# Starting attention's first head inside the last two iterations of a Mamba and expert stage

## The reference, cut to what matters

```
x = _layernorm(x + _L0_attn_ref(x, ...), axis=-1)     # Mamba
x = _layernorm(x + _L0_ffn_ref(x, ...), axis=-1)      # router, 4 experts, top 2
x = _layernorm(x + _L1_attn_ref(x, ...), axis=-1)     # softmax(scores) @ v, 16 heads
x = _layernorm(x + _L1_ffn_ref(x, ...), axis=-1)
```

## Time and profile before

| what | us |
|---|---|
| median of 3 runs (lowest, highest) | 3949.27 (3946.3, 3962.15) |
| the profiled execution | 3957.01 |
| its span, first to last instruction | 3955.2 |
| TensorE busy (share) | 3451.3 (87%) |
| VectorE busy (share) | 2949.9 (75%) |
| ScalarE busy (share) | 2202.5 (56%) |
| GpSimd busy (share) | 1519.5 (38%) |
| mean granted TensorE clock, as a share of full speed | 0.934 |

### The profile page before, as it was taken

How to read it: one execution, slowest core, us unless ns; L and a number is a source line. 1 busy time by engine, 2 the same in 40 slices (tenths; PEclk the granted TensorE clock), 3 DMA queues, 4 the chain that set the end, 5 groups by cost and what they waited for, 6 DMA issues and landing times. The chain is left out here.

```text
span 3955.2 us, 50070 instructions
## 1 busy us (share of the span) xinstructions
PE 3451.3 (87%) x14561; PEld 1589.3 (40%) x14561; DVE 2949.9 (75%) x3567; ACT 2202.5 (56%) x3624; POOL 1519.5 (38%) x1292
## 2 busy tenths in 40 slices
PE   3348888898888889898958999999999999999898
PEld 1115545454554545455621233333223323233566
DVE  3898787888878787884128888888878888888343
ACT  4436555555556545554112777777777777777221
POOL 1988778787777878786010000000000000000110
PEclk8669999898999989999976999999999999999999
DMA  2111213121121312212103000000000000001000
GB/s 97 31 38 48 62 55 106 56 86 67 59 67 56 106 54 76 75 58 103 51 32 96 21 18 18 18 18 18 18 18 18 20 23 19 18 18 34 21 28 30
DMA packets 110953, 183.09 MB, mean 46 GB/s; under 512 B 14624, under 2 KB 84792, under 8 KB 102010
## 3 DMA queue, kind: packets, MB, share of 16 engines
q1 hardware_dynamic: 110713, 180.20, 14.3%
HBM read 154.05 MB, written 26.09 MB: 46 GB/s over the span
## 5 line engine op out<-in xcount | busy, mean ns | idle before, releaser
L1700 DVE TENSOR_REDUCE tile_max<-ps 128x1 f32<-128x1024 f32 x1076 | 1267.7, 1220 | 254.7 <-PE ps L1483 251.9
L1641 ACT ACTIVATE probs<-ps 128x512 f32<-128x512 f32 x2056 | 1116.2, 599 | 457.0 <-PE ps L1497 431.3
L1182 POOL TENSOR_TENSOR h<-h,c_sb 128x512 f32<-128x512 f32 x512 | 684.8, 1369 | 329.8 <-DVE state L996 329.7
L990 DVE TENSOR_TENSOR_SCAN h<-decay,state,ps 128x512 f32<-128x512 f32 x512 | 655.1, 1279 | 105.9 <-POOL y_sum L1193 34.1
L1497 PE MATMUL ps<-qs,ks 101*128 101x512 bf16 x2056 | 708.4, 382 | 1.2
L1483 PE MATMUL ps<-ks,qs 99*128 99x512 bf16 x2152 | 664.0, 390 | 49.0 <-DMA ks<-scratch_kb 41.1
L1193 POOL TENSOR_TENSOR y_sum<-y_sum,h 128x512 f32<-128x512 f32 x512 | 638.6, 1279 | 8.7 <-issue 0.2
L1817 POOL COPY vh<-v_all 128x256 f32 (+1 forms) x32 | 12.6, 400 | 1403.4 <-PE ps L1507 1339.8
L1507 PE MATMUL ps<-probs,vh 128*32 128x512 f32 x4096 | 545.6, 605 | 3.5 <-issue 3.5
L539 PE MATMUL ps<-x1T,e_w 128*128 128x512 f32 x1024 | 486.4, 626 | 58.5 <-ACT hid L807 58.5
L561 PE MATMUL ps<-e_w,hid 128*128 128x256 f32 x2048 | 455.4, 381 | 38.4 <-issue 19.0
(11 more groups left out here) (176 smaller groups left out, 2870.7 us busy)
## 6 DMA issues: line engine op xcount, KB each, us to landing
e_w<-in_e_w SPq DMA_DIRECT2D x64, 1024.0 KB, 7.0
c_sb<-scratch_c SPq DMA_DIRECT2D x128, 256.0 KB, 3.3
qs<-scratch_q SPq DMA_DIRECT2D x210, 64.0 KB
ks<-scratch_k SPq DMA_DIRECT2D x210, 64.0 KB
scratch_q<-parts SPq DMA_DIRECT2D x16, 384.0 KB, 4.0
scratch_k<-parts SPq DMA_DIRECT2D x16, 384.0 KB, 4.1
xr<-scratch_x SPq DMA_DIRECT2D x10, 512.0 KB, 4.2
xn_tok<-in_x SPq DMA_DIRECT2D x8, 512.0 KB, 4.9
```

The lines of the kernel that those rows point to most:

```text
L990: v.tensor_tensor_scan(h[:, n % 2, m, :], decay[:, n % 2, m, :], ps[:, 0, :], state[:, n, m:m + 1], ALU.mult, ALU.add).then_inc(s["h_ready ...
L1182: last = nc.gpsimd.tensor_tensor(h[:, n % 2, m, :], h[:, n % 2, m, :], c_sb[:, n % C_RING, :], ALU.mult)
L1641: fn(probs[:, step % 2, qc, :], ps[:, S_BANK[i], :], ACT.Exp)\
L1700: v.tensor_reduce(tile_max[:, t, half:half + 1], ps[:, slot(side):slot(side) + PAIR, :].rearrange("p a n -> p (a n)"), AX.X, ALU.max).then ...
```

## The change

A class `Shared` holds buffers and semaphores for both stages. `decay`, `delta` and `du` of the first stage lie in the memory of the stacks, `h`, `xb` and `pre` in that of the values, `y_sum` in that of the staged values. In iterations 8 and 9, where their first use is over, the second stage's run-up is done: VectorE fills the stacks' last rows (slot 3 of iteration 8), SyncE loads three stacks and the values of sequence 0 (slot 5), GpSimd stages the values of four heads (slot 8), and the 49 items are done by TensorE and VectorE in the numbers that `START` gives per slot: 34 in slots 8 to 15 of iteration 8, and 3, 4, 2 and 6 in slots 2, 3, 4 and 9 of iteration 9. In `up` and `down` TensorE places one item behind each output block or group; elsewhere they stand at the slot's end. On VectorE they stand at the slot's end always. They use one pair of banks (2 and 3) where the run-up used two. Item 36 is the turn, and `load_neg` for head 0 stands in slot 5 of iteration 9. The second stage then starts with `step_of(0, ...)`.

```diff
+START = {(NCH, 8): 6, (NCH, 9): 6, (NCH, 10): 6, (NCH, 11): 4, (NCH, 12): 2, (NCH, 13): 2, (NCH, 14): 4,
+         (NCH, 15): 4, (NCH + 1, 2): 3, (NCH + 1, 3): 4, (NCH + 1, 4): 2, (NCH + 1, 9): M_FIRST - 43}
+START_BANK = 2
...
-        delta = sb("delta", [P, DB, CH])
-        du = sb("du", [P, DB, CH])
+        delta = blocks_of[:, 2 * CH * DB:3 * CH * DB].rearrange("p (b t) -> p b t", b=DB)
+        du = blocks_of[:, 3 * CH * DB:].rearrange("p (b t) -> p b t", b=DB)
...
         @block.sync
+                    if n == 5 and isinstance(i, int) and i == chunks:
+                        first_loads()
+                    if n == 5 and isinstance(i, int) and i == chunks + 1:
+                        load_neg(sp, sh, scr, s["passed_sp"], 0, 0)
                     if n == 8 and inside(q):
                         store_parts(q, 0, "q")
...
+            def first_loads():
+
+                sp.wait_ge(sh.sems["setup"], 2)
+                for name, n in (("q", 2), ("k", 2), ("kb", 1)):
+                    sp.wait_ge(s[name + "_stored"], 16 * n * CB)
+                for u in range(3):
+                    load_stack(sp, sh, scr, u, u)
+                sp.wait_ge(s["y_added"], chunks * NS)
+                sp.wait_ge(s["v_stored"], 16 * CB)
+                load_values(sp, sh, scr, 0)
...
         @block.tensor
+            def start_head(k):
+
+                first = sh.sems
+                if k == 0:
+                    pe.wait_ge(s["bx_ready"], chunks * NS * DB)
+                at_least(pe, first["max_read"], k)
+                if k == TURN_0:
+                    pe.wait_ge(first["max_ready"], 1)
+                    nc.tensor.transpose(ps[0:KT, START_BANK, 0:P], sh.row_max[:], ident[:]).then_inc(first["max_mm"], 1)
+                    return
+                t, half = divmod(k - (k > TURN_0), PAIR)
+                j, row = divmod(t, KT)
+                if row == 0 and half == 0:
+                    pe.wait_ge(sh.stack_loaded[j], STACK_DMAS)
+                for i in range(PAIR):
+                    at = PAIR * half + i
+                    last = mm(ps[:, START_BANK + i, :], sh.qs[0:K_MAX, j, row * P:(row + 1) * P],
+                              sh.ks[0:K_MAX, j, at * CH:(at + 1) * CH], start=True, stop=True)
+                last.then_inc(first["max_mm"], 1)
...
@@ up(c, e, half), behind each of its four output blocks
                     full(last, key)
+                    spare()
@@ down(c, e, pair), behind each of its two groups
-                last.then_inc(s["down_mm"], 1)
+                    if i == 1:
+                        last.then_inc(s["down_mm"], 1)
+                    spare()
@@ iteration(i), TensorE, end of slot n
+                    while quota[0] > 0:
+                        spare()
...
         @block.vector
+            def set_stacks():
+
+                dve.wait_ge(s["h_ready"], chunks * NS * DB)
+                v.memset(sh.qs[STACK:, :, :], 1.0).then_inc(sh.sems["setup"], 1)
+                v.memset(sh.ks[STACK:, :, :], 1.0).then_inc(sh.sems["setup"], 1)
@@ iteration(i), VectorE, end of slot n
+                    if n == 3 and isinstance(i, int) and i == chunks:
+                        set_stacks()
...
+                    for _ in range(START.get((i, n), 0) if isinstance(i, int) else 0):
+                        start_head(begun[0])
+                        begun[0] += 1
...
         @block.gpsimd
+            def first_values():
+
+                pool.wait_ge(s["g_ready"], chunks)
+                nc.gpsimd.memset(sh.vh[:, :, :, HD:], 0.0).then_inc(sh.sems["ones_set"], 1)
+                pool.wait_ge(sh.sems["ones_set"], 1)
+                nc.gpsimd.memset(sh.vh[:, :, :, HD:HD + 1], 1.0).then_inc(sh.sems["ones_set"], 1)
+                pool.wait_ge(sh.sems["v_loaded"], 16)
+                for j in range(ROT):
+                    stage_values(nc, sh, j, 0, j)
...
@@ attention_ffn, SyncE
-            sp.wait_ge(s["setup"], 4)
-            sp.dma_start(ident[:], a["ident"]).then_inc(s["loads"], 16)
-            for u in range(3):
-                load_stack(u, u, None)
-            for b in range(B):
+            for b in range(1, B):
+                load_values(sp, sh, scr, b)
...
@@ attention_ffn, TensorE
-            pe.wait_ge(s["loads"], 16)
-            n = 0
-            for t in range(PRE_TILES):
-                for half in range(PAIR):
-                    max_pair(n, n % 2, 0, t // KT, t % KT, half)
-                    n += 1
-                if n == TURN_0:
-                    turn_max(n, n % 2, 0)
-                    n += 1
+            n = M_FIRST
             step_of(0, 0, 0, 0, n, n % 2)
```

More of the change, by code:

```diff
@@ L122, in ln_buffers @@
             sb(name + "_t", [P, TT])[:])
+HEADS = B * NH
+QC = L // CH
+KT = L // P
+STEP = QC
+PER_HEAD = KT * STEP
+PAIR = 2
+S_BANKS = 3
+S_BANK = [i % S_BANKS for i in range(PER_HEAD - 4)] + [0, 1, 0, 1]
+M_AT = 3
+AV_BANK = 7
+PRE_TILES = KT + KT // 2
+TURN_STEP = KT // 2
+FOLD_STEP = 1
+M_PER_HEAD = PAIR * KT + 2
+TURN_0 = PAIR * (KT + 2)
+M_FIRST = PAIR * PRE_TILES + 1
+M_BASE = M_FIRST - 1
+CREDIT = S_BANKS + 1
+ROT = 4
+STACK = 6 * HD
+K_MAX = STACK + 3
+K_ALL = K_MAX + 2
+VW = 2 * HD
@@ new lines, with __init__, sb, sem @@
+Q_PARTS = (0, 0, 1, 0, 2, 1)
+K_PARTS = (0, 1, 0, 2, 0, 1)
+STACK_DMAS = 16 * (2 * 6 + 1)
+START = {(NCH, 8): 6, (NCH, 9): 6, (NCH, 10): 6, (NCH, 11): 4, (NCH, 12): 2, (NCH, 13): 2, (NCH, 14): 4,
+         (NCH, 15): 4, (NCH + 1, 2): 3, (NCH + 1, 3): 4, (NCH + 1, 4): 2, (NCH + 1, 9): M_FIRST - 43}
+START_BANK = 2
+class Shared:
+    def __init__(self, nc, ctx):
+        def sb(name, shape, dt=F32):
+            return ctx.enter_context(nc.sbuf_tensor(name, shape, dt))
+        def sem(name):
+            return ctx.enter_context(nc.semaphore(name))
+        self.ident = sb("ident", [P, P])
+        self.stacks = sb("stacks", [P, 2 * ROT * L], BF16)
+        self.qs = self.stacks[:, 0:ROT * L].rearrange("p (j t) -> p j t", j=ROT)
+        self.ks = self.stacks[:, ROT * L:].rearrange("p (j t) -> p j t", j=ROT)
+        self.vals = sb("vals", [P, B * KT * D])
+        self.v_all = self.vals[:].rearrange("p (t n) -> p t n", n=D)
+        self.heads_v = sb("heads_v", [P, ROT * KT * VW])
+        self.vh = self.heads_v[:].rearrange("p (j t n) -> p j t n", j=ROT, t=KT)
+        self.tile_max = sb("tile_max", [P, KT, PAIR])
+        self.row_max = sb("row_max", [P, KT])
+        self.neg = sb("neg", [KT, P])
+        self.neg_parts = sb("neg_parts", [KT, 2, P], BF16)
+        names = "v_loaded max_mm max_read max_ready neg_steps neg_stored v_staged setup ones_set".split()
+        self.sems = {n: sem(n) for n in names}
+        self.stack_loaded = [sem(f"stack_loaded{j}") for j in range(ROT)]
+        self.neg_loaded = [sem(f"neg_loaded{j}") for j in range(ROT)]
@@ new lines, in load_stack @@
+def load_stack(sp, sh, scr, head, j):
+    rows = bass.ds(head * HD, HD)
+    for i in range(6):
+        for dst, name, part in ((sh.qs, "q", Q_PARTS[i]), (sh.ks, "k", K_PARTS[i])):
+            sp.dma_start(dst[i * HD:(i + 1) * HD, j, :].rearrange("p (j t) -> p j t", t=CH),
+                         scr[name][rows, :, part, :]).then_inc(sh.stack_loaded[j], 16)
+    sp.dma_start(sh.ks[STACK:K_MAX, j, :].rearrange("p (j t) -> p j t", t=CH),
+                 scr["kb"][bass.ds(head, 1), :, :, :].rearrange("o j p t -> p (o j) t"))\
+        .then_inc(sh.stack_loaded[j], 16)
@@ L1275, in iteration @@
                         add_edge(f)
+                    if n == 8 and isinstance(i, int) and i == chunks:
+                        first_values()
                     if 4 <= n < 8 and inside(q):
@@ L1284, in _ @@
             iterations(pool, iteration)
[L1287 to L1311, removed]
 def earlier(i):
@@ L1386, in attention_ffn @@
         s = {n: sem(n) for n in names}
-        stack_loaded = [sem(f"stack_loaded{j}") for j in range(ROT)]
-        neg_loaded = [sem(f"neg_loaded{j}") for j in range(ROT)]
+        s.update(sh.sems)
+        stack_loaded, neg_loaded = sh.stack_loaded, sh.neg_loaded
         x2_loaded = [sem(f"x2_loaded{j}") for j in range(2)]
-        STACK_DMAS = 16 * (2 * 6 + 1)
         block = ctx.enter_context(nc.Block())
@@ L1812, in stage @@
             def stage(u, b, hd, j):
-                free = (u - ROT + 1) * KT
-                wait_alone(pool, s["passed_pool"], s["av_mm"], free)
-                column = bass.ds(hd * HD, HD)
-                nc.gpsimd.tensor_copy(vh[:, j, :, 0:HD],
-                                      v_all[:, bass.ds(b * KT, KT), bass.ds(hd * HD, HD)])\
-                    .then_inc(s["v_staged"], 1)
-            pool.wait_ge(s["setup"], 4)
-            pool.wait_ge(s["v_loaded"], 32)
-            for j in range(ROT):
-                stage(j, 0, j, j)
+                wait_alone(pool, s["passed_pool"], s["av_mm"], (u - ROT + 1) * KT)
+                stage_values(nc, sh, j, b, hd)
             with pool.Fori(1, quads) as quad:
@@ L1935 @@
```

(6 more changed lines are left out.)

143 lines of the change are left out of this document (69 added, 74 removed).

## The result

The changed kernel takes 3903.2 us (median of 4 runs, 3902.4 to 3904.5), where the kernel before, run four times now, has a median of 3955.7. The ratio is 0.9872, with a 95% interval of 0.9851 to 0.9892, so it is 1.3% faster. The forecast was 3905.

A forecast was written before the change was run, and what follows sets the result against it. TensorE bounds late iteration 8; between the stages a run-up of 86.4 us holds up heads and first stage. Less 41.7 us of costs in iterations 8 and 9, border and heads' start, 44.7 is won: 3949.3 becomes 3905, range 3890 to 3928.

The forecast's parts named there:

- run-up removed: Between the stages: two fills, stack DMAs and 49 items, 86.4 us in which nothing of heads or first stage moves.
- iteration 8, 34 items: Among the expert matmuls: 0.43 us of TensorE per item plus stalls at late sums, +15.3 us (13.3 to 20.7).
- slot 3, 4 items: Iteration 9: TensorE free 6.2 us later, a wait of 0.82 covered, +5.3 us.
- slot 4, 2 items: Iteration 9: VectorE's product for the keys stands behind item 42, 4.6 us instead of 1.57, +3.0 us.
- slot 9, 6 items: Iteration 9: items behind the bias split move the stage's end by +8.0 us (6.0 at full clock).
- clock in iteration 9: Iteration 9: q and k projections at full clock, 3.8 us of cross matmuls at half; +4 us (0 to +17).
- border: Start of the second stage: TensorE needs issue time for its first instructions, +2.0 us (0.3 to 5).
- The covers: Iteration 8: fills, SyncE's loads and GpSimd's staging fit idle time and cost nothing; SyncE's slack about 5 us.
- the fills would take GpSimd's access to memory: Rival, iteration 8: fills slow GpSimd's norm scale, up to 13.8 us, so 3919; chance 0.07.
- No change: Rival: items in `up` miss their cover, each costing 1.92 us instead of 0.43; 50.7 us more, 3955; chance 0.04.
- Slower by a clock that falls in iteration 8: Rival: bf16 items between f32 work lower the clock, up to 120 us, so 4025; chance 0.03.
- A cheaper end of iteration 9: Rival: full clock and a quick border at the end of iteration 9, 3894; chance 0.10.

The follow-up runs named there:

- layout alone: Changed kernel's shared buffers kept, but fills, loads and items back in the second stage; ratio to before 0.9995, again 1.0000 (3957.4 us).
- the third set: The changed kernel run a third time, unaltered, beside the layout alone; 3914.6 us (5 runs), ratio to before 0.9891.
- those of the second: The changed kernel run a second time, unaltered; 3910.3 us (4 runs), ratio to before 0.9882.
- items_last: Changed kernel with the 34 items of iteration 8 moved to the last slot of iteration 9; 3972.2 us (6 runs), ratio to before 1.003.
- best2: Changed kernel with items also in slots 6 and 7 of iteration 8, three under chunk 7's norm, one each in slots 3 and 9; 3887.0 and 3892.2 us.

## Why the prediction was right

The forecast of 44.7 us won stands against 44.1 from the profiles of one pattern (layout alone and change), 42.8 and 45.8 from the medians of the third set (against the layout and against before), 46.8 from those of the second, and 50.6 as the ratio of the first four runs gives it (52.5 as the plain difference of the medians). The last is too much by the scatter: the runs of before spread over 17 us by themselves. The range of 3890 to 3928 holds all 13 runs.

By its terms, each against the layout alone:

| term | predicted | measured |
|---|---|---|
| run-up removed | 86.4 | 85.8 |
| iteration 8, 34 items | 15.3 | 17.0 |
| slot 2, 3 items | 3.1 | 3.0 |
| slot 3, 4 items | 5.3 | 6.0 |
| slot 4, 2 items | 3.0 | 4.5 |
| slot 9, 6 items | 8.0 | 8.7 |
| clock in iteration 9 | 4 | 1.0 by itself, the rest in the rows above |
| border | 2.0 | 0.2 |
| low clock at the heads' start | 1 | 1.2 |

The measured column is the difference of the distances between the same instructions in both traces, as 169.8 - 152.8 = 17.0 for the start of the last `down`s behind `gated`. Both traces are in the short form.

The mechanism of every large term is as forecast, but that the costs add up to 41.6 where 41.7 stood is luck in part: iteration 8 was 1.7 us short, and the border 1.8 too long.

- *Iteration 8.* The forecast had the mechanism and each stall. Items stood 2.15 us apart with no wait, the late sums showed as 0.48 and 2.19 us. The extra 1.7 us goes with a short stretch at half clock late in iteration 8, right behind the matmuls of `base` (the experts' bias), which have four contraction rows:

```profile
1986.48 1.99 PE L684 MATMUL ps<-e_b,cwT 4*128 4x256 f32 x8
1988.40 2.76 PE L694 MATMUL ps<-x1T,e_w 128*128 128x512 f32 x4
1990.95 1.06 PE L561 MATMUL ps<-stacks 99*128 99x512 bf16 x2
```

The expert block and the item took 2.76 and 1.06 us instead of 1.88 and 0.60. The four-row matmuls don't bring this on by themselves. In the trace of before they stand in the same place, and sixteen rows behind them ran at full clock:

```profile
1982.67 1.99 PE L529 MATMUL ps<-e_b,cwT 4*128 4x256 f32 x8
1984.59 7.13 PE L539 MATMUL ps<-x1T,e_w 128*128 128x512 f32 x16
```

So it is in both traces of the layout alone and in that of items_last, which have no items there, while all nine traces with items in iteration 8 have the stretch at half clock. The items set it off at this place; by what mechanism stays open. The prediction's sum held no clock term for iteration 8.
- *The covers* (fills, SyncE's queue, GpSimd) cost nothing, as forecast. SyncE issued the stacks from 1862.0 to 1886.9 and the weight load followed at 1890.7, before it was due. That the fills would take GpSimd's access to memory is refuted for the split: its subtractions beside the second fill took 2.13 us as always. The norm's scale, at which the rival aimed, was over 0.1 us before the first fill, so its own steps were not put beside one. The Trainium skill (SBUF — State Buffer, Who interferes with whom) states that a VectorE instruction with at most one SBUF input, outside the two-port modes, doesn't contend with GpSimd, and the trace agrees for a fill, 6.88 and 2.13 us side by side.
- *Iteration 9.* The clock's term was put in one sum and came in pieces: 0.7 us in slot 3, 1.5 in slot 4, 1.0 at the key bias and 0.7 in the last slot come on top of the items' own. That is 3.9 us where 4 stood. Of the eight cross matmuls behind the four items only the first four ran at half clock, 3.62 us instead of 1.94, where all were assumed to; the rest of the 3.9 us lies in items, in the matmuls of `soft` (3.01 us instead of 1.98) and in the key bias. So the size of this term is right by more than one error.
- *The border* was over-sized: TensorE starts 0.25 us after the stage is let go, not 2.0. The 1.6 us of issue time belong to the fill, in whatever place it stands (1.76 and 1.65 us in iteration 8).
- *The rivals.* No change: refuted by the items 2.15 us apart with no wait, and items_last shows the price of 2.3 us where the cover is missing and so how much the cover is worth. Slower by a clock that falls in iteration 8: it stayed at 0.98, and the one dip cost 1.7 us. A cheaper end of iteration 9: the border was quick, but the clock was not full.

What stays open: which pattern the loop of iterations falls into in a given execution, and why the spread of the runs is some 16 us. That it isn't the change is shown by the layout alone, which has the short form once and the long form once; that it is the clock is only argued, from the granted clock that goes with it (0.66 or 0.83 in iteration 8).

## What to carry to other kernels

Work that needs little of a busy engine and much of an idle one is cheapest as single pieces between the busy engine's own blocks: an item cost TensorE 0.43 us there, 0.50 with the late sums and the dip of the clock, and 2.3 us in a row of its own. What has to be compared is the distance between two pieces against the round trip through the other engine (2.15 us against 1.92 here), and which sums of the other engine's list now stand behind them. Pieces put into the tail, where every engine waits for every other, cost their whole round trip, and a second pair of banks or a place further up wins part of that back.

## What the runs showed of the hardware that was not expected

- A fill of 32 x 8192 bf16 elements on VectorE had 1.6 to 1.8 us of issue time before it, both fills in the trace of before and both in that of after, at the start of a stage and in the middle of one; GpSimd's fill of 128 x 1024 (0.95 us) had none.
- Behind matmuls of four contraction rows the clock stayed at full in the four traces without items around them (7.13 us for sixteen rows), and fell to half for a while in the nine with items (2.76 us instead of 1.88 for the next four rows, a granted clock of 0.91 over 20 us).
- Two bf16 matmuls of an item put between f32 matmuls cost their own 0.43 us and nothing for the change of type: the next f32 block started 0.44 us after the item in iteration 8.
- The first scores began 0.25 us after the end of the stage in which TensorE had work until the end, and just as soon in best2, where it had been idle for 11.9 us before.
